# A graph kernel's opening stage on one core: 28 gathered units set beside word counts, look-ups and edge sums in another rhythm

## The reference

```python
def _edge_conv(x, src, dst, edge_attr, W, b, denom):
    msg = concatenate([x[src], edge_attr], axis=1) @ W + b
    s = segment_sum(msg, dst, num_segments=x.shape[0])
    return s / denom[:, None]

counts = segment_sum(ones(E), dst, N); denom = maximum(counts, 1.0)
h = _edge_conv(x, src, dst, edge_attr, W0, b0, denom)
outputs = [h]
for W, b in ((W1, b1), (W2, b2), (W3, b3)):
    z = _edge_conv(concatenate(outputs, axis=1), src, dst, edge_attr, W, b, denom)
    outputs.append(z)
return layernorm(x + outputs[-1])
```

## Time and profile before

| | us |
|---|---|
| three runs | 1377.53, 1379.7, 1382.56 |
| median | 1379.7 |
| the profiled execution | 1375.91 |
| its span, first to last instruction | 1374.2 |

### The profile page before, as it was taken

One profiled execution on the slowest core, in us unless ns is written; L12 is line 12 of the kernel. 1 busy time (PEld: TensorE's weight loads), 2 busy tenths in 40 slices (PEclk: granted clock), 3 DMA queues, 4 the chain that ended last, 5 costly groups with the idle time before them and its releaser, 6 DMA issues.

```text
span 1374.2 us, 15435 instructions
## 1 busy us (share of the span) xinstructions
PE 560.1 (41%) x3020; PEld 420.2 (31%) x3020; DVE 766.1 (56%) x2933; ACT 444.0 (32%) x1066; POOL 804.9 (59%) x766
## 2 busy tenths in 40 slices
PE   2354553466665577776266500000045410665000
PEld 1344442344443334443155400000034410555000
DVE  7676555778874533332398564121176875786630
ACT  7453442223222333343144233000034422343530
POOL 6887665335452456665677466566577702775376
PEclk9655565556668878898676655555567765777555
DMA  2576987911112568776767657665567759674311
GB/s 59 179 256 221 299 280 253 354 45 35 35 28 91 186 230 273 260 267 215 275 217 247 206 171 274 206 202 162 153 228 253 260 158 300 231 268 137 124 52 37
DMA packets 157594, 265.36 MB, mean 193 GB/s; under 512 B 22672, under 2 KB 91367, under 8 KB 157472
## 3 DMA queue, kind: packets, MB, share of 16 engines
q1 hardware_dynamic: 112128, 149.57, 32.2%
q0 software_dynamic: 26240, 59.55, 15.6%
q10 hardware_dynamic: 19104, 54.92, 10.8%
HBM read 114.39 MB, written 149.75 MB: 192 GB/s over the span
## 4 chain that ended last, share of the span: by engine, by line
DVE 28%; issue 18%; PE 16%; POOL 14%; DMA 13%; another core or an unknown queue 4%; ACT 3%; DVEq 2%; SPq 1%; POOLq 0%; ACTq 0%
POOL out_rows L715 4%; DVE stat L1376 4%; PE hp L1722 4%; POOL G L638 3%; DVE area L1201 3%; PE segp L1722 3%; DVE area L1391 3%; POOL G L673 3%; DMA area<-z_of_nodes 2%; DVE area L1127 2%; DVE area L1221 2%; PE hp L1764 2%; ACT area L866 1%; PE segp L1764 1%
## 5 line engine op out<-in xcount | busy, mean ns | idle before, releaser
L638 POOL DMA_INDIRECT G<-x_in,srci x196 | 222.1, 1133 | 161.0 <-PE segp L1634 80.9
L653 POOL DMA_INDIRECT z_of_nodes<-area,sum_rows x144 | 142.3, 988 | 106.2 <-issue 55.5
L866 ACT ACTIVATE area<-area,shift,rs 128x128 f32<-128x128 f32 x390 | 153.3, 480 | 17.4 <-DVE shift L1398 16.0
L1758 PE MATMUL segp<-ZERO 128*128 128x384 f16 (+1 forms) x54 | 22.2, 410 | 320.6 <-DVE EC L1412 278.6
L859 ACT ACTIVATE sd<-dev,eps 128x13 f32<-128x13 f32 x30 | 9.2, 306 | 409.6 <-DVE dev L1384 382.1
L681 POOL DMA_INDIRECT G<-part_rows,s0r x70 | 77.4, 1106 | 81.7 <-DMA part_rows<-UT 56.9
L1758 PEld LDWEIGHTS segp<-ZERO 128*128 128x128 f16 x54 | 6.1, 112 | 324.4 <-DVE EC L1412 304.5
L1764 PE MATMUL segp<-G,EC 128*128 128x128 f32 (+1 forms) x432 | 81.7, 350 | 51.6 <-DMA G<-h_rows,dsti 17.2
L681 POOL DMA_INDIRECT G<-part_rows,previ x70 | 78.0, 1114 | 37.0 <-issue 19.2
L841 ACT ACTIVATE area<-segp,zero,inv 128x512 f32<-128x512 f32 x72 | 54.4, 776 | 136.8 <-PE segp L1722 61.4
L681 POOL DMA_INDIRECT G<-h_rows,dsti x70 | 80.1, 1145 | 30.0 <-issue 19.9
(11 more groups left out here) (398 smaller groups left out, 1551.1 us busy)
## 6 DMA issues: line engine op xcount, KB each, us to landing
part_rows<-area SPq DMA_DIRECT2D x36, 1024.0 KB
z_of_nodes<-ZERO ACTq DMA_DIRECT2D x28, 1024.0 KB
area<-x_in SPq DMA_DIRECT2D x30, 832.0 KB
area<-z_of_nodes SPq DMA_DIRECT2D x30, 832.0 KB
out_rows<-area ACTq DMA_DIRECT2D x30, 832.0 KB
part_rows<-ZERO SPq DMA_DIRECT2D x56, 256.0 KB
h_rows<-area SPq DMA_DIRECT2D x36, 258.0 KB
part_rows<-UT SPq DMA_DIRECT2D x60, 128.0 KB
```

The costliest lines, as they stand in the source:

```text
L638: g.indirect_dma_start(G[:, slot, 0:D], None, x, bass.IndirectOffsetOnAxis(ap=srci[:, c:c + 1].bitcast(u32), axis=0), bounds_check=last_no ...
L653: g.indirect_dma_start(ZF, bass.IndirectOffsetOnAxis(ap=sum_rows[:, c:c + 1], axis=0), HS3[:, b, j, 3 * D + 1:4 * D + 1], None, bounds_che ...
L866: last = a.activation(XL[:, b, k], XL[:, b, k], ACT.Identity, bias=shift[:, b, r:r + 1], scale=rs[:, b, r:r + 1])
```

## The change

Three numbers of PE's order change, and the place of 16 of the 28 clearing stores:

- word chunks: five behind each of units 0 to 5 (before: four behind 0 to 6);
- look-ups: four behind each of units 6 to 12 (before: three behind 7 to 16);
- edge and list chunks: two behind each of units 13 to 26 (before: three behind 17 to 26);
- clearing stores: behind `x_out` of units 0 to 5 and 13 to 20 (before: 0 to 13), two each as before.

```diff
+LOOK_UNIT, EDGE_UNIT = 6, 13
...
+            clear_at = [*range(LOOK_UNIT), *range(EDGE_UNIT, EDGE_UNIT + IT - LOOK_UNIT)]
+
             def clear_sums(u):
                 for q in (0, 1):
-                    e.dma_start(zfill[2 * u + q], ZERO[:, :].unsqueeze(1).to_broadcast([P, ZROWS // CG, CW])).then_inc(s["cleared"], 16)
+                    e.dma_start(zfill[2 * clear_at.index(u) + q], ZERO[:, :].unsqueeze(1).to_broadcast([P, ZROWS // CG, CW])).then_inc(s["cleared"], 16)
...
-                if u < 14:
+                if u in clear_at:
                     clear_sums(u)
...
-                if u < 7:
-                    for c in range(u * 4, u * 4 + 4):
+                if u < LOOK_UNIT:
+                    for c in range(u * 5, min(u * 5 + 5, UNITS)):
                         word_sums(c)
-                    if u == 6:
+                    if u == LOOK_UNIT - 1:
...
-                elif u < 17:
-                    for c in range((u - 7) * 3, min((u - 6) * 3, UNITS)):
+                elif u < EDGE_UNIT:
+                    for c in range((u - LOOK_UNIT) * 4, min((u - LOOK_UNIT + 1) * 4, UNITS)):
                         look_up(c)
-                    if u == 16:
+                    if u == EDGE_UNIT - 1:
...
-                    for c in range((u - 17) * 3, min((u - 16) * 3, UNITS)):
+                    for c in range((u - EDGE_UNIT) * 2, min((u - EDGE_UNIT + 1) * 2, UNITS)):
                         edge_chunk(c)
                         list_chunk(c)
```

## The result

| | before | after |
|---|---|---|
| median, us (4 runs each) | 1378.96 | 1363.72 |
| lowest to highest | 1377.53 to 1382.56 | 1363.06 to 1366.2 |
| the profiled execution | 1375.91 | 1366.2 |
| its span | 1374.2 | 1364.5 |

The ratio is 0.9885, with a 95% interval of 0.9859 to 0.9911: 15 us less. The forecast was 1365.7, 14 less. The sum came out right; its terms didn't.

A forecast was written before the change was run, and what follows sets the result against it. Look-ups were taken to wait for broadcast loads, edge chunks to be bound by DVE. 1375.9 - 37 (earlier edge chunks) + 16 (block 2) + 7 (register loads) = 1361.9; median 3.8 higher, 1365.7 us; range 1345 to 1386.

The forecast's parts named there:

- Word stage: Word chunks at the front: one x unit less saves 7 us, look-ups starting at 114.2 instead of 121.4.
- The fear that denser chunks would slow every gather: Word chunks: DVE's two-port mode could slow all seven gathers to 1.98 us, taking back some 4 of 7 us.
- Look-up stage: Look-ups, to the last pick: from 106.6 us to 77, with the clearing stores moved away and four look-ups a group.
- the group of 9.8 us: Look-ups: a group of four takes 9.8 us, with PE's short register load; six groups are 58.7 us.
- the half of 12.4 us for waits without a holder: Look-ups: two waits of unknown holder total 12.4 us; half, 6 us, was kept since nothing tied them to stores.
- First edge chunk: End of look-ups and DVE's small steps: first edge chunk at 214 instead of 251, 37 us earlier.
- (a) Block 2 late: Edge chunks: block 2's feature loads, behind fills and moved stores, arrive late; DVE stands 16 us, bounds 0 and 30.
- no collision: Rival: block 2's loads at the edge chunks cost no wait; 30 us less in all, 1350 us; chance 0.25.
- (b) Dearer register loads: Edge chunks: DVE's register loads take longer under full DMA, 7 us more in all, between 2 and 14.
- PE in the edge stage: Edge chunks: fourteen x units in place of ten add PE work but cost nothing, since PE idles there.
- the slow one: Rival: the broadcast load's round trip, not stores, sets look-ups, groups 13.9 us; 1391 us; chance 0.14, with more wait at block 2.
- Given back in full: Rival: at 300 GB/s the wait at block 2 is 30 us, cancelling the gain; 1380 us; chance 0.18.

The follow-up runs named there:

- C: Third chip's first set of runs: kernel before 1367.6 us, the change unaltered 1348.2 us, ratio 0.9845.
- e5: Changed kernel with four word chunks behind x units 0 to 6, as before, later stages one x unit later; 1358.2 us, ratio 0.9916 to before.
- B: Another chip's set of four kernel variants; kernel before took 1330.4 us there, without a trace, and the changed kernel was not run.
- e1: New rhythm alone, all clearing stores behind x units 0 to 13 as in the kernel before; 1315.1 us, ratio 0.9881 to before.
- A: First comparison, chip unknown: kernel before 1379.0 us, changed kernel 1363.7 us, ratio 0.9885.
- e2: Kernel before with only the stores moved, behind x units 0 to 6 and 17 to 23; 1328.7 us, ratio 0.9980 to before.
- e3: Changed kernel with the second half of the stores behind x units 19 to 26 instead of 13 to 20; 1301.1 us, ratio 0.9784 to before.
- D: Third chip's second set of runs: kernel before 1369.8 us, the change unaltered 1348.5 us, ratio 0.9861.
- e6: Changed kernel with late stores, seven look-ups behind x units 6 to 9, edge chunks over 10 to 27; 1361.1 us, ratio 0.9962 to before.
- e4: Changed kernel with block 2's feature loads set among SP's fills instead of behind them; 1302.2 us, ratio 0.9798 to before.
- e8: Changed kernel with all 28 look-ups behind x unit 6, edge chunks over 7 to 27, stores behind 15 to 22; 1383.7 us, ratio 1.0078 to before.

## Why the prediction was right, and where it wasn't

**Word stage: 7 said, 12.2 measured** (11.1 on C, 10.0 in time by e5). The term was mis-sized. I let x unit 3 begin at 75.0 and it began at 72.39; from there to x unit 5 I counted 24.6 us, and it took 22.4: a group of five is 11.2 us, 9.9 for the chunks and 1.3, not 2.4, for what nothing covers. The last group took 14.5, as worked out. The fear that denser chunks would slow every gather was half borne out: six of seven gathers in x unit 3's set were stretched (1.52 to 1.68 us), five in unit 4's, three and one of 1.25 in unit 5's, and the first two sets took 13.0 and 12.7 us, more than the 12.5 that I had worked out; yet PE waited for no gather from 60 to 110 us. The prediction took for this the rule that a DVE instruction in two-port mode shuts GpSimd out (the Trainium skill, SBUF - State Buffer, Who interferes with whom). The word chunks are TENSOR_TENSORs, which by the same section have no two-port mode and, with both inputs in SBUF, contend with GpSimd's reads; the trace agrees only that single gathers are stretched beside them.

**Look-up stage: 77 us said, 86.4 measured.** The mechanism is shown on B: there the stores held up the broadcast loads (e1). The failing step is the group of 9.8 us. On B it is 9.1, on A 11.1, since the slow stretch at each seventh gather takes 3 us that I had no term for. B's 66.6 and A's 86.4 us stand on both sides of my 77; the half of 12.4 us for waits without a holder was a guess, and it was luck that it landed between them. I had also left out POOL's seven gathers, 9.1 us a unit: with three look-ups (e2) this floor rules, and with four it is just reached. In e3 POOL never pauses, its sets take 9.1 to 9.4 us and the x units come 9.1 apart; no product waited for a gather, but a faster DVE alone would soon be held by it.

For A and C a rival to my mechanism stands. Those waits of before are likely slow stretches: on A they end at 214.06 and 222.60, and the seventh gathers of units 16 and 17 went out at 212.07 and 221.27; in C two waits of 6.0 and 5.7 us end 2.0 and 0.7 us behind theirs. The last clearing stores had gone out at 191.8 (190.6 in C), so no store explains them, and PE's products for the first had run by 209. Since the other pauses of before end at the same place, and x units are 11 us apart there with stores and three look-ups and in after without stores and with four, much of what I put to late loads may be the stretch. The gain of the stage is then three x units fewer in it, and what the moved stores bring there is open: e1's kernel was not run in A, C or D.

**First edge chunk: 37 us earlier said, 32.5 measured** (34.7 on C): 5.2 us more in the word stage and 9.8 less in the look-ups.

**(a) Block 2 late: 16 said, 5.6 measured** on A (the step from chunk 7 to chunk 8 took 13.3 us, and 7.7 with a split and no wait), 8.1 on C, 4.1 on D. The collision is there and the rival "no collision" is refuted, but the term was a difference of two large numbers. Data at 88 us behind the fills' start, wanted at 72, I had said; it came at 82 and was wanted at 78. The queues' traffic from 191 to 274 us (packets, MB, share of the 16 engines):

```profile
q1 hardware_dynamic: 16608, 18.84, 66.9%
q10 hardware_dynamic: 4224, 8.39, 28.3%
q0 software_dynamic: 992, 2.03, 6.8%
```

29.3 MB, where I had counted 30.6, at 354 GB/s, where I had 351. And the fills began 27 us ahead of the first edge chunk instead of 23; on B, without slow stretches, e3_stores_late has 27 too, so the 23 was simply too short. An error of 6 us in each of two numbers of 80 took most of the term.

**(b) Dearer register loads: 7 said, 8.0 measured** (177.9 - 164.3 - 5.6; 6.0 on C). It is what is left of the edge stage, but its main part is read directly: chunks 4 to 6 take 1.3 to 1.4 us more each than before, and the two loads of a chunk take some 0.95 us each there, in place of 0.30. The load of L1208 from 219 to 262 us, shortest, median and longest in ns, is the row to set against the earlier trace rows:

```profile
L1208 DVEq TENSOR_LOAD <-c0r x6: 632/975/1055, 224.1 to 258.9; - x6
```

**PE in the edge stage: nothing, as said.** e1's 163.8 us with 14 x units (B) against 164.3 with 10 (A) speaks for it, across two chips. With 18 (e6) the stage is 21 us longer than c_after's, with gaps between PE's products that no term of mine has.

**The sum.** At the step: 12.2 + 20.2 + 0.1 - 5.6 - 8.0 = 18.9, against 7 + 30 - 16 - 7 = 14. The four errors are +5, -10, +10 and -1, and cancel to +5; that the forecast came within 2 us of the median is luck in good part, of these errors and of the stretch behind the step. Of the rivals, the slow one was rightly held small: without stores hardly a look-up waits for its load, in e3 not one. "Given back in full" would have taken a rate of 300 GB/s.

## What to carry to other kernels

A stage where several engines work in a ring has a floor from each of them; after taking a cost away from the one that waits, work out the period of every other member (here seven gathers, 9.1 us) before pricing the gain, and expect two edits that each remove one of two such limits to give little alone and more together (of the look-ups on B some 0 and 8 us apart, 26 in one, by estimate). Bulk stores cost what stands beside them, not their own issue: set them where nobody waits for a small load on the same DMA engines, and look for the next bulk transfer that they will meet there. A term that is the difference of two times of 80 us deserves a range of its own, and the order in the issuing engine's list (one small load ahead of the bulk) may remove it (e4).

## What was not expected of the hardware

- DVE's small instructions started 0.7 us apart, not 0.24, for some 3 us around every seventh indirect gather on POOL, in every profile of the new rhythm in A, C and D but in none on B; with POOL idle it did not happen in 47 us (e8). In e6 and e8 the products of PE's edge chunks had such gaps too, 23.5 and 23.7 us in all.
- One register load on DVE took 0.30 us with quiet DMA engines and 0.98 in the median under 370 GB/s; PE's load ahead of an x unit, 0.54 us in the median over the kernel, took 1.58 to 1.88 there.
- The four feature loads of 56 KB issued among 18 MB of fills landed in time (e4), while the same loads issued behind them came 11 us after their issue.
- The stretch behind the step behind the edges, with the same instructions in all kernels, took 927 to 930 us on chip B and 950 to 968 in the other sets.
